# An attention and feed-forward block behind a recurrent scan: another order inside the head step, the V split moved, gate and residual in one VectorE pass

## What is computed

```python
# x [16, 128, 256], cond [16, 256]
x = x + GRU(h0=cond, inputs=x)                   # 128 sequential steps, D = 256
# then one transformer block, conditioned on cond (16 heads of 128, MLP 1024):
shift1, scale1, gate1, shift2, scale2, gate2 = split(cond @ ada_w + ada_b, 6)
x1 = ln(x) * (1 + scale1) + shift1
q, k, v = split(x1 @ qkv_w + qkv_b)
attn = softmax(q @ k.T * 128 ** -0.5)
y = x + gate1 * (attn @ v @ out_w + out_b)
x2 = ln(y) * (1 + scale2) + shift2
x = x + y + gate2 * (gelu(x2 @ ffn_w1 + ffn_b1) @ ffn_w2 + ffn_b2)
```

## Time and profile before

| | |
|---|---|
| time, median of 3 runs | 756.67 us (756.54 to 760.99) |
| profiled execution | 760.32 us, span 758.5 us |
| TensorE busy | 718.8 us, 95% |
| VectorE busy | 532.8 us, 70% |
| ScalarE busy | 470.0 us, 62% |
| GpSimd busy | 289.6 us, 38% |
| mean granted TensorE clock | 0.984 |

### The profile page before, as it was taken

The page is one execution under the profiler, slowest core; times in us unless marked ns, Lnnn a source line. Parts: engine busy times, 40 slices in busy tenths (PEclk is TensorE's granted clock), DMA queues, the critical chain, the costliest instruction groups (busy, mean ns, idle before and its releaser), DMA issues.

```text
span 758.5 us, 23585 instructions
## 1 busy us (share of the span) xinstructions
PE 718.8 (95%) x9324; PEld 498.7 (66%) x9324; DVE 532.8 (70%) x1423; ACT 470.0 (62%) x1621; POOL 289.6 (38%) x326
## 2 busy tenths in 40 slices
PE   6899999999999999799999999999999999999997
PEld 5688999899999976455555555555555555544555
DVE  5667666666676676377777889778897888834643
ACT  4445556655655555467667766776667677666453
POOL 0222222222222220554454466555665646520040
PEclk9889999999999999899999999999999999999999
DMA  6221444344433425444343345544433444310001
GB/s 233 94 80 45 128 113 115 101 127 122 119 101 93 110 69 119 120 106 91 98 98 98 84 88 89 92 100 88 91 98 85 93 90 98 87 27 28 29 2 56
DMA packets 116262, 70.17 MB, mean 93 GB/s; under 512 B 72075, under 2 KB 108087, under 8 KB 116151
## 3 DMA queue, kind: packets, MB, share of 16 engines
q1 hardware_dynamic: 115575, 67.09, 36.0%
q10 hardware_dynamic: 576, 1.57, 0.6%
HBM read 32.98 MB, written 18.87 MB: 68 GB/s over the span
## 4 chain that ended last, share of the span: by engine, by line
PE 78%; DVE 12%; ACT 4%; issue 3%; DMA 2%; POOL 0%; SPq 0%; DVEq 0%; ACTq 0%
PE bank L526 18%; PE bank L528 17%; PE bank L527 17%; PE bank L631 11%; PE bank L546 5%; PE bank L639 5%; DVE nmx L1323 3%; ACT prob L1048 2%; DVE mx L1320 2%; DVE prob L1329 1%; DVE four L1339 1%; DVE xn L1314 1%; PE bank L533 1%; DVE h_hi L1250 1%; DMA pT_lo<-p_lo 1%
## 5 line engine op out<-in xcount | busy, mean ns | idle before, releaser
L1048 ACT ACTIVATE prob<-bank,nmx 128x128 f32<-128x128 f32 x256 | 90.5, 368 | 76.9 <-DVE nmx L1323 76.9
L486 POOL TENSOR_TENSOR p_lo<-prob,p_hi 128x512 f16<-128x512 f32 x64 | 74.7, 1168 | 154.2 <-ACT p_hi L1041 150.9
L631 PE MATMUL bank<-h_hi,whh_hi 128*128 128x16 f16 x1536 | 111.6, 174 | 6.9 <-DVE h_hi L1250 6.6
L432 POOL TENSOR_TENSOR w_lo<-stage,w_hi 128x320 f16<-128x320 f32 x64 | 52.1, 814 | 155.4 <-DVE h_lo L1255 152.9
L631 PE MATMUL bank<-h_hi,whh_lo 128*128 128x16 f16 x1536 | 108.8, 172 | 0.4 <-issue 0.4
L631 PEld LDWEIGHTS bank<-h_hi,whh_hi 128*128 128x128 f16 x1536 | 92.7, 97 | 17.3 <-DVE h_hi L1250 16.1
L526 PE MATMUL bank<-y_hi,w_hi 128*128 128x512 f16 x248 | 94.8, 382 | 3.6 <-DVE four L1334 3.4
L527 PE MATMUL bank<-y_hi,w_lo 128*128 128x512 f16 x248 | 94.3, 380 | 0.0
L528 PE MATMUL bank<-y_lo,w_hi 128*128 128x512 f16 x248 | 94.2, 380 | 0.0
L631 PEld LDWEIGHTS bank<-h_hi,whh_lo 128*128 128x128 f16 x1536 | 91.3, 97 | 1.1 <-issue 0.7
L1238 DVE TENSOR_TENSOR_SCAN npre<-zr,bank 128x64 f32<-128x64 f32 x128 | 36.7, 287 | 58.8 <-ACT zr L993 57.3
(11 more groups left out here) (153 smaller groups left out, 2158.4 us busy)
## 6 DMA issues: line engine op xcount, KB each, us to landing
v_spill<-v_rows SPq DMA_DIRECT2D x32, 512.0 KB, 3.9
v_full<-v_spill SPq DMA_DIRECT2D x64, 256.0 KB, 2.9
stage<-in_weights SPq DMA_DIRECT2D x16, 640.0 KB, 4.1
x<-in_x SPq DMA_DIRECT2D x16, 128.0 KB, 4.0
out<-xr SPq DMA_DIRECT2D x3, 512.0 KB, 3.1
xr<-in_ada_r SPq DMA_DIRECT2D x1, 1024.0 KB, 7.7
pT_hi<-p_hi SPq DMA_TRANSPOSE x64, 2.5
pT_lo<-p_lo SPq DMA_TRANSPOSE x64, 2.5
```

The lines of the kernel that those rows point to most:

```text
L432: gtt(w_lo[:, j * PC:(j + 1) * PC], stage[:, r % 2, i * PC:(i + 1) * PC], w_hi[:, j * PC:(j + 1) * PC], sub).then_inc(piece_lo, 1)
L486: gtt(p_lo[:, d % 2, :], flat_prob[d % 2], p_hi[:, d % 2, :], sub).then_inc(p_l, 1)
L631: nc.tensor.matmul(out(m0 + m), half[:, k, (m0 + m) * P:(m0 + m + 1) * P], h_hi[:, k * B:(k + 1) * B, 1], start=False, stop=False, skip_gr ...
L1048: op = nc.scalar.activation(prob[:, d % 2, j, :], bank[3][:, j * T:(j + 1) * T], ACT.Exp, bias=nmx[:, j:j + 1], scale=SCALE, accum_out=den ...
```

## The change

1. **V's last items.** The items of the last two blocks are made in pairs of heads, block 14 and block 15 by turns. A new `store_last(pair)` stores each pair by itself, and `load_values` waits for its own pair.
2. **TensorE.** The step becomes keys(d), attend(d-3), project_out(d-4), queries(d+1), scores(d): `attend` is three heads back and not two, and stands in front of the projection. `v_hi` and `v_lo` get four buffers for three.
3. **VectorE.** The step becomes score_max(d-1), query_low(d), the group's work, softmax(d-1), key_low(d), attend_low(d-3).
4. **ScalarE.** `attend_high(d-3)` goes in front of `prob_high`.
5. **GpSimd.** `value_split(d+1)` waits until `nmx` of head d is written (`s_nm`); then GpSimd waits for the multiplied probabilities (`s_pn`), does the group's work, and `prob_low(d)` at the end of the step.
6. **Gate and residual.** `gate_out` and its tile are gone. GpSimd adds the gated bias `gbo` to `xr_v` a group ahead (`bias_first`, in steps 2 and 3); `residual` is one VectorE instruction per sequence and half, projection in PSUM times gate plus `xr_v`, in steps 4 to 7. So that the later bias is right, `gb2` is lessened by `gbo` once.
7. **SP.** `load_values(d+2)` is issued in front of `turn(d)`.

```diff
-    order += [(NBL - 2, pair) for pair in range(PAIRS // 2)] + [(NBL - 1, pair) for pair in range(PAIRS // 2)]
-    order += [(NBL - 2, pair) for pair in range(PAIRS // 2, PAIRS)]
-    order += [(NBL - 1, pair) for pair in range(PAIRS // 2, PAIRS)]
+    order += [(NBL - 2, 0), (NBL - 2, 1), (NBL - 1, 0), (NBL - 1, 1)]
+    order += [(n, pair) for pair in range(2, PAIRS) for n in (NBL - 2, NBL - 1)]
...
-GATE, RESIDUAL = {4: 0, 6: 1}, {5: 0, 7: 1}
+FIRST, RESIDUAL = {2: 0, 3: 1}, {4: 0, 5: 1, 6: 2, 7: 3}
...
+            def store_last(pair):
+
+                scalar, vector = taken(VITEMS.index((NBL - 1, pair)))
+                sp.wait_ge(v_act, scalar)
+                sp.wait_ge(v_dve, vector)
+                side, at = pair // (PAIRS // 2), pair % (PAIRS // 2) * VP
+                for n in (NBL - 2, NBL - 1):
+                    sp.dma_start(v_spill[n * BS:(n + 1) * BS, :, pair * VP:(pair + 1) * VP].rearrange("t b c -> b t c"),
+                                 v_rows[:, n % 2, side, at:at + VP]).then_inc(v_last[pair % 4], 16)
...
+            prob_low(0)
             value_split(0)
-            for d in range(HEADS):
+            value_split(1)
+            pool.wait_ge(ada_ok, 4)
+            for d in range(1, HEADS):
                 g, i = d // H, d % H
-                prob_low(d)
                 if d + 1 < HEADS:
+                    pool.wait_ge(s_nm, d + 1)
                     value_split(d + 1)
-                if d >= H and (d + 1) % H == VAR:
-                    norm_rstd(d // H - 1)
+                pool.wait_ge(s_pn, d + 1)
+                if i in FIRST:
+                    bias_first(g, FIRST[i])
+                if g > 0 and i + 1 == VAR:
+                    norm_rstd(g - 1)
...
+                prob_low(d)
...
             for d in range(LAG, HEADS):
                 g, i = d // H, d % H
                 keys(d)
+                attend(d - 3)
                 project_out(d - LAG)
...
-                attend(d - 2)
                 scores(d)
 
+            attend(HEADS - 3)
             project_out(HEADS - 4)
             up(1)
-            up(2)
             attend(HEADS - 2)
             project_out(HEADS - 3)
+            up(2)
             up(3)
...
-            def residual(g, pair):
-                two = slice(2 * pair, 2 * pair + 2)
-                b = slice(g * QUAD + 2 * pair, g * QUAD + 2 * pair + 2)
-                dve.wait_ge(o_gated, KD * g + pair + 1)
+            def residual(g, j):
+                b = g * QUAD + j
+                if j == 0:
+                    dve.wait_ge(o_mm, g + 1)
+                    dve.wait_ge(first_ok, KD * (g + 1))
                 for k in range(KD):
-                    op = tt(by_block(xr2[:, k, b, :]), by_block(gated[:, k, two, :]), xr_v[:, k, b, :, :], ALU.add)
+                    op = stt(xr2[:, k, b, :].rearrange("p (n t) -> p n t", t=BS),
+                             out_bank(g, k)[:, j * T:(j + 1) * T].rearrange("p (n t) -> p n t", t=BS),
+                             ada[:, G1 + k, b:b + 1], xr_v[:, k, b, :, :], ALU.mult, ALU.add)
                 op.then_inc(o_res, 1)
```

More of the change, by code:

```diff
@@ L149, in build @@
         v_full = sb("v_full", [P, 2, N])
-        v_hi = sb("v_hi", [P, 3, N], f16)
-        v_lo = sb("v_lo", [P, 3, N], f16)
+        v_hi = sb("v_hi", [P, 4, N], f16)
+        v_lo = sb("v_lo", [P, 4, N], f16)
         mx = sb("mx", [P, QUAD])
@@ L377, in load_values @@
                 g, head = d // H, d % H
+                if d < H:
+                    sp.wait_ge(v_last[head // 2 % 4], 32 * (head // (2 * 4) + 1))
                 if d > 1:
@@ L741, in pair_rows @@
             def pair_rows(g, pair):
-                pe.wait_ge(o_res, KD * g + pair + 1)
-                if pair == 0:
-                    pe.wait_ge(o_gated, KD * (g + 1))
+                pe.wait_ge(o_res, QUAD * (g + 1))
                 for i in range(2 * KD):
@@ L814, in attend @@
                     c = slice(j * T, (j + 1) * T)
-                    mm = product(bank[5][:, c], (v_hi[:, d % 3, c], v_lo[:, d % 3, c]),
+                    mm = product(bank[5][:, c], (v_hi[:, d % 4, c], v_lo[:, d % 4, c]),
                                  (pT_hi[:, d % 2, j, :], pT_lo[:, d % 2, j, :]), j == 0, True)
@@ L871, in _ @@
             tall_parts(tall_rest, 1, 1, last).then_inc(k_mm, 1)
-            for i in range(VTAIL + 5, VTAIL + 7):
-                value_item(i)
+            value_item(VTAIL + 6)
             scores(0)
@@ L890, in _ @@
             keys(3)
+            attend(0)
             value_item(VTAIL + 17)
@@ L1114, in _ @@
                     query_high(d + 1)
-                attend_high(d - 2)
-                if g > 0 and i in GATE:
-                    for k in range(KD):
-                        gate_out(g - 1, k, GATE[i])
                 if g > 0 and i in HIGH:
@@ L1121, in _ @@
             softmax(HEADS - 1)
+            attend_high(HEADS - 3)
+            prob_high(HEADS - 1)
             feed_forward(0)
-            prob_high(HEADS - 1)
             attend_high(HEADS - 2)
@@ L1221, in modulation_gates @@
                        ).then_inc(ada_ok, 1)
+                dve.wait_ge(ada_ok, 3)
+                tt(gb2[:, :, :], gb2[:, :, :], gbo[:, :, :], ALU.subtract).then_inc(ada_ok, 1)
             def value_out(i):
@@ L1402, in _ @@
                 query_low(d)
-                attend_low(d - 3)
-                softmax(d - 1)
-                key_low(d)
                 if g > 0:
@@ L1416, in _ @@
                         norm_modulate(g - 1, MODULATE[i])
+                softmax(d - 1)
+                key_low(d)
+                attend_low(d - 3)
             score_max(HEADS - 1)
+            softmax(HEADS - 1)
             attend_low(HEADS - 3)
-            softmax(HEADS - 1)
             feed_forward(0)
@@ L1428, in _ @@
                     sum_group(t // FM - 1, range(2 * (t % FM), 2 * (t % FM) + 2))
-                elif t == FM + 2:
-                    for pair in range(2):
-                        residual(NG - 1, pair)
+                elif FM + 2 <= t < FM + 4:
+                    for j in range(2 * (t - FM - 2), 2 * (t - FM - 2) + 2):
+                        residual(NG - 1, j)
                 elif t == ROWS_AT:
```

72 lines of the change are left out of this document (33 added, 39 removed).

## The result

The changed kernel takes **727.88 us** (median of 4 runs, 727.21 to 728.90) against 756.61 (4 runs, 756.16 to 760.99): ratio 0.961, 95% interval 0.957 to 0.965. The forecast was 727.0, range 719 to 742. The profiled execution took 728.36, span 726.6, mean granted clock 0.993. Executions of the kernel before differ by up to 4 us, and the longer ones show a lower clock: of the 28 timed beside the experiments the nine above 758.4 all had a mean granted clock of 0.983 to 0.986, of the other 19 only four; the profiled one (760.32) had 0.984.

A forecast was written before the change was run, and what follows sets the result against it. TensorE's own instructions set the floor; the loop lost 26.4 us above it. Loop 24.2, start 8.4 and end -1.0 gave 31.6 us less: 728.7 from the profiled execution, 725.1 from the median, middle 727, range 719 to 742.

The forecast's parts named there:

- The floor: TensorE's own instructions in the 60 loop steps: 5.22 us each plus 5.3 for row transposes, 318.5 us.
- Split behind `nmx`: GpSimd casts V only after `nmx`, so neither split op holds it; the 0.96 us goes from every step that had it.
- VectorE's new order: Group work moves into the hole between low q and `rden`; only the variance costs, 0.5 us a group, 1.5 for three.
- The modulation: VectorE group work of two to four ops, under 1.3 us, taken as covered by the hole before `rden`.
- the spare of the chain: In a step without loss the chain is ready 0.33 us before the next scores; some 0.2 of it is real.
- Residual from PSUM: VectorE's residual reads PSUM and one SBUF tensor; cost bounded at 0 to 3 us over 12 steps, taken as 0.
- First steps: V loads still queue behind the pair stores; 0.7 us put for this together with GpSimd's group work.
- the sums of rests: GpSimd's longest group job, 1.326 us before `p_lo`; can touch the next `nmx` by some 0.2 in six steps.
- rival A: The V split meets VectorE's multiply by 0.63 us, costing 0.3 in each of 60 steps: 18 us, so 745; chance 0.15.
- The start: Earlier V removes TensorE's 5.92 us wait before attend(0) and 2.75 of slow clock: 8.7 less 0.3, so 8.4 us.
- The end: attend(62) waits for head 61's low half, on VectorE behind the last softmax; costs 1.0 us.
- The level: 31.6 us less gives 728.7 from the profiled execution or 725.1 from the median; the middle, 727, was taken.

The follow-up runs named there:

- e2: The kernel before with one line added: GpSimd waits for the next head's scaled maximum before that head's V split; 735.73 us, ratio 0.971.
- e1: The changed kernel without GpSimd's wait for the scaled maximum before the V split; 730.20 us, ratio 0.964.
- e12: The kernel before with an unused 128x4 GpSimd clear, and a wait for it, between `v_hi` and `v_lo`; 741.27 us, ratio 0.978.
- e7: The changed kernel with the old residual: ScalarE writes a gated copy, VectorE adds two SBUF tensors behind the low half of q; 729.79 us, ratio 0.963.
- e9: The changed kernel with the last softmax behind attend_low(61), variance sums one step earlier and stores of V pairs later; 727.34 us, ratio 0.960.
- e8: The kernel before with the scaled maximum `nmx` computed on ScalarE instead of VectorE, V split ungated; 738.69 us, ratio 0.975.
- e13: The changed kernel without V pairs and with attend(0) right behind scores(2); 731.33 us, ratio 0.966.

## Why the prediction was right, step by step

- **The floor.** 5.22 a plain step, 5.66 with row transposes: both to 0.01. The 60 steps lie 3.1 over 318.5, 2.2 by the sum.
- **Split behind `nmx`.** 0.17 in every step from step 4 on, and this alone (e2) is the loop's gain of 24. Right in mechanism and size. What the forecast did not see: the loss hung on 0.05 us between two starts (e1, e12), so the new order removes it a second time. The argument "the gate is what saves the changed kernel", which is e1's forecast, missed by some 13 us.
- **VectorE's new order.** Forecast 1.5 for the variance, else nothing: 0.40 x 3 = 1.2. The modulation, taken as covered, is a little too long for the hole: its four instructions start at 449.24, `rden` follows only at 450.52, some 0.25 late, and the scores come 0.05 late, once a group. Here is the variance in the timelines of VectorE and GpSimd, `mean` held to the end of `v_lo` as forecast:

```profile
427.42 1.03 DVE L1302 TENSOR_SCALAR mean<-part 128x4 f32<-128x4 f32 x1
...
427.26 1.16 POOL L516 TENSOR_TENSOR v_lo<-v_full,v_hi 128x512 f16<-128x512 f32 x1
```

  The multiply comes 0.62 late there and the scores 0.40, so the spare of the chain is 0.22, as taken.
- **Residual from PSUM**, 0 taken of 0 to 3: no step is late by it. The rule of the Trainium skill ("SBUF — State Buffer", "Who interferes with whom") that the forecast cited beside it now has a row for this form: 0.34 each, also under `v_lo`. The old form at this place would have cost 2.4 (e7).
- **First steps**, 0.7 taken with the sums of rests: 1.6 measured in the first steps alone, and nothing at the sums of rests: the one term mis-sized. Steps 4 and 6 are 0.91 and 0.70 late: on SP, V's load stands behind the pair stores (store 305.35, load 306.62), the split of head 4 starts only at 310.31 and the multiply meets it; e9, which moved the stores, moved the late steps too.

```profile
311.04 1.66 DVE L1338 TENSOR_TENSOR prob<-prob,rden 128x512 f32<-128x512 f32 x1
...
311.00 1.16 POOL L516 TENSOR_TENSOR v_lo<-v_full,v_hi 128x512 f16<-128x512 f32 x1
```

  That is rival A's mechanism, in two steps of 60. In the others the overlap is 0.12 and costs nothing.
- **The start**, 8.4 forecast, 8.4 measured; but the working credited it to V's pairs, 6.7 us earlier, with the later attend(0) as cover. V does come as early as forecast (by 296: the first split starts at 295.48 without a wait, before it waited for V until 302.75). But the runs give pairs 3.5, `p_lo` in front of the split more, the later attend(0) nothing that can be told. The sum was right because together these end the gap and the half clock behind it; the share of each was not. The match to 0.1 is in part luck: with the old order this stretch took 26.57 to 27.62 in the four kernels that have it.
- **The end**, 1.0 forecast: the gap is 0.95, the stretch 0.8 longer.
- **The level.** 31.6 less was forecast on the profiled spans, 31.9 came, 1.0 of it ahead of scores(0), where scatter alone can make it. The medians differ by 28.7, since the profiled execution of before stood 3.7 over its median and that of after 0.5. The sum from the profiled execution, 728.7, lies 0.8 above the result, the sum from the median, 725.1, lies 2.8 below, and the middle that was taken, 727, 0.9 below. Nothing in the working told which level the result would be at, so a match within 1 us is luck. Why the levels differ stays open.

## What to carry to other kernels

When two engines that can block each other run in one loop, write down the start of each blocking pair to 0.1 us: a loss that comes in every second step can be a sign that the two start together, as here. Then set their order by a semaphore rather than by phase, and do that alone first: here one line gave 21.7 us and the whole change 28.7, and the loop of the whole change is no shorter than with that line alone. A nudge that moves both of them tests nothing.

When a gap has several covers, undo them one by one before saying which one worked.

## What the runs showed of the hardware

- A VectorE instruction of 4 elements a partition with its source in SBUF is held to the end of a GpSimd instruction that started 0.05 earlier (1.13 for 0.17), and not if it starts 0.09 (e1) or 0.12 (e12) ahead of it, in e12 even though GpSimd's 0.10 clear was still running for its first 0.04. On ScalarE the same work took 0.20 under `v_lo` (e8).
- The multiply of two SBUF tensors took 1.66 where it started 0.04 behind `v_lo`, and its usual 0.69 where `v_lo` ended 0.12 behind the multiply's start.
- Of two residual adds of two SBUF tensors the one that started 0.14 behind `v_lo` took 1.38, the one in front of it 0.41; with one source in PSUM each took 0.34 (e7, after).
- Behind a TensorE gap of 5.92 and of 6.40 (e2) the granted clock was 0.50 (the 1.2 GHz level) for about 5.5 us; behind a gap of 2.54 (e13) it stayed at 1.00. So the shorter gap cost less than its share.
